# v spread over the key rows by transfers through DRAM, six banks in the ring, scores four tiles at a time

## The chip, the cores and the metric

One core of one Trainium2 chip runs the whole program. The metric is the device time of one execution in microseconds (us). TensorE multiplies matrices (PE in the rows, its weight loads PEld), VectorE (DVE), ScalarE (ACT) and GpSimd (POOL) do elementwise work, and SyncE (SP) issues all the transfers.

## The reference

32 sequences of 128 tokens with 512 features go through two layers. The first is cross attention with 32 query heads and 8 key heads of 16 features; the second is a linear-recurrence layer (RWKV) with 32 heads of 16 features and a feed-forward part. Cut to what matters:

```python
# layer 0
q = x @ Wq + bq;  k = ctx @ Wk + bk;  v = ctx @ Wv + bv
scores = einsum('bkgld,bksd->bkgls', q, k) / sqrt(16) + mask
out = einsum('bkgls,bksd->bkgld', softmax(scores), v)
x = layernorm(out @ Wo + bo + x) * gamma + beta
# layer 1: token shift, low-rank mixes, then
w = exp(-exp(time_decay + tanh(x5[1] @ decay_w1) @ decay_w2))
r, k, v = x5[3] @ Wr.T, x5[0] @ Wk.T, x5[2] @ Wv.T;  g = silu(x5[4] @ Wg.T)
def step(s, rkvw):                       # over 128 tokens
    a = k_t[:, :, :, None] * v_t[:, :, None, :]     # per head 16 x 16
    out = einsum('bhk,bhkd->bhd', r_t, u * a + s)
    return a + w_t[:, :, :, None] * s, out
att = groupnorm(outs);  x = x + (att * g) @ Wo.T
x = x + sigmoid(xr @ Wfr.T) * (square(relu(xk @ Wfk.T)) @ Wfv.T)
```

## The kernel before, in words

The batch is cut into 16 groups of two sequences (T = 256 tokens together). The work of a group is cut into steps such as `score.4` or `outer.7`; each engine has a written-out list of its steps (`PE_ORDER`, `ACT_ORDER`, `POOL_ORDER`, `DVE_ORDER`, lines 121 to 158), and runs the list once in each round. A step with `+1` or `+2` belongs to the group that entered one or two rounds earlier, so attention of one group, recurrence of the one before it, and output and feed-forward part of the one before that lie side by side. There are 16 + 2 rounds. Engines wait for one another by semaphores; within an engine the list is the order.

The recurrence keeps, for every head, a 16 x 16 state. 128 partitions hold 8 heads x 16 key rows (a chunk, four of them); along the free axis lie value columns d and the 256 tokens. A unit is one chunk and four value columns, so there are 16 units in a group. A unit goes through a slot of `st`, 128 x 1024, of which there are four:

- `spread` (TensorE, L717): v of one value column and head must stand in all 16 key rows of the head. A matmul with a 0/1 matrix `sel` does it. It runs in a faster number type that keeps fewer bits, so v is split into two parts: ScalarE writes the rounded v to `v_hi` (L979), VectorE the rest to `v_lo` (step `proj_v`, L1276), and eight matmuls a unit add both in `bank_pair`, two of the eight PSUM banks. Unit u's spread waits until the product of unit u-1 has read the pair.
- `outer` (VectorE, L1215): `st` slot = pair x k. `first` (ScalarE, L1027) writes the incoming state into the first column of each sequence.
- `scan` (VectorE, L1226, four scans), `weigh` (L1236, times r), then `reduce` (TensorE, L740), which sums over key rows for two units at once and counts `summed`. With that count the two slots are free.
- `readout` (L1244, L1246) adds the bonus term r·k·u·v; v for it is put together from both parts by GpSimd (L1089). `rk` is its step too (L1085).

The attention: `score.n` (L566) makes two score tiles in two PSUM banks on two sets of 32 rows of the array, four matmuls; VectorE takes each tile's row minima (L1173), ScalarE the exponential (L862), `turn_p` turns it (L575), `values` multiplies (L585), `inverse`, `flip`, `share`, `gather` and `project` finish. `low`, `low_rank`, `mix` (L1267 on VectorE, L1102 on GpSimd), `tdecay`, `decay` make the five mixes; `proj_r`, `proj_k`, `proj_v`, `proj_g` (L696) project them.

PSUM: `psum_jobs` hands the banks of `RING` (0, 1, 2, 4) out in the order of TensorE's list; bank 3 holds the attention's value sums, bank 7 the readout, and the pair is the rest. A step that writes a bank waits until its last reader is through. SP's transfers stand in `turn`: in each round `load_c`, `load_s` 0 and 1, `store`, `bring`, `load_s` 2, `save`, `load_m`, `load_x`, `load_t`, `load_s` 3.

Of the kernel before, what the change touches and what calls it, by code (L numbers as in the profile page):

```python
# [55 lines left out]
SLOTS = 4  # L56
# [65 lines left out]
reduce.4+2 spread.12+2 low_rank.0+1 spread.13+2 key.0 reduce.5+2 tdecay.0+1 spread.14+2 low_rank.2+1 proj_r.0+1  # L122
spread.15+2 decay.0+1 proj_v.0+1 proj_k.0+1 spread.0+1 reduce.6+2 decay.1+1 value.0 spread.1+1 reduce.7+2 query.0
spread.2+1 var.0+2 proj_r.1+1 score.0 rstd.0+2 query.1 score.2 spread.3+1 proj_g.0+1 proj_g.1+1 turn_p.0 turn_p.1
turn_p.2 reduce.0+1 spread.4+1 score.4 out.0+2 turn_p.3 score.6 spread.5+1 turn_p.4 out.1+2 values.0 reduce.1+1
turn_p.5 score.8 spread.6+1 proj_v.1+1 turn_p.6 flip.0 proj_k.1+1 turn_p.7 turn_m.0+2 score.10 share.0 spread.7+1
# [6 lines left out]
state.0+1 state.1+1 key.0 first.14+2 tdecay.0+1 proj_v.0+1 decay.0+1 first.15+2 proj_r.0+1 first.0+1 proj_k.0+1  # L133
decay.1+1 first.1+1 square.1+2 query.0 first.2+1 proj_r.1+1 state.2+1 score.0 score.1 state.3+1 query.1 score.2
proj_g.0+1 proj_g.1+1 turn_p.0 first.3+1 score.3 turn_p.1 row2.0+2 turn_p.2 first.4+1 score.4 turn_p.3 norm2.0+2
score.5 score.6 first.5+1 turn_p.4 score.7 norm2.1+2 first.6+1 turn_p.5 row0.0 apply2.0+2 score.8 apply2.1+2
first.7+1 flip.0 proj_v.1+1 score.9 turn_p.6 proj_k.1+1 turn_p.7 turn_m.0+2 share.0 score.10 turn_p.8 score.11
turn_p.9 score.12 turn_p.10 score.13 score.14 turn_p.11 score.15 turn_m.1+2 turn_p.12 turn_p.13 flip.1 turn_p.14
turn_p.15 share.1 first.8+1 norm0.0 apply0.0 first.9+1 norm0.1 first.10+1 norm1.0 apply0.1 first.11+1 ffn_k.0+2
norm1.1 apply1.0 ffn_k.1+2 apply1.1 ffn_r.0+2 square.0+1 turn_n.0 turn_n.1 ffn_r.1+2 row1.0 low.0 first.12+1  # L140
keep_row.0 first.13+1
# [3 lines left out]
norm0.0+1 rk.2+2 affine0.0+1 norm0.1+1 affine0.1+1 norm1.0+1 norm1.1+1 mix.0+1 mix.1+1 mix.2+1 mix.3+1 rk.3+2 rk.0+1  # L145
mix.4+1 negate.0 norm2.0+2 rk.1+1 norm2.1+2 bias.0 bias.1
# [3 lines left out]
outer.12+2 mix.0+1 mix.1+1 outer.13+2 scan.12+2 mix.2+1 mix.3+1 outer.14+2 readout.2+2 weigh.12+2 outer.15+2  # L150
scan.13+2 scan.14+2 proj_v.0+1 weigh.13+2 scan.15+2 weigh.14+2 outer.0+1 weigh.15+2 mix.4+1 value.0 outer.1+1
readout.3+2 scan.0+1 var.0+2 score.0 outer.2+1 score.1 weigh.0+1 groupnorm.0+2 score.2 scan.1+1 outer.3+1 score.3
proj_g.0+1 weigh.1+1 scan.2+1 proj_g.1+1 scan.3+1 weigh.2+1 score.4 score.5 outer.4+1 out.0+2 scan.4+1 score.6
weigh.3+1 score.7 outer.5+1 out.1+2 scan.5+1 score.8 readout.0+1 score.9 inverse.0 outer.6+1 weigh.4+1 proj_v.1+1
scan.6+1 score.10 score.11 weigh.5+1 outer.7+1 score.12 score.13 gather.0 weigh.6+1 score.14 outer.8+1 score.15
# [16 lines left out]
LATEST = max(late for t in (PE_STEPS, ACT_STEPS, POOL_STEPS, DVE_STEPS) for _, _, late in t)  # L172


RING, READOUT = [0, 1, 2, 4], 7


def psum_jobs():

    jobs, turn = [], 0  # L180
    for name, n, late in PE_STEPS:
        keys = [(name, n)]
        if name == "low_rank":
            keys = [("mix", 2 * m + p) for p in range(2) for m in range(n, min(n + 2, len(MIX)))]
        elif name == "score":
            keys = [(name, n), (name, n + 1)]
        elif name == "decay":
            keys = [("decay", n)] + [("mix", 8 + m) for m in range(2 * n)]
        elif name == "rstd":
            keys = [("rstd", 0), ("rstd", 1)]  # L190
        elif name == "reduce":
            keys = []
            if n % 2 == 0:
                jobs.append((("readout", n // 2), READOUT, late))
        elif name in ("spread", "values"):
            keys = []
# [6 lines left out]
def build(nc, x, ctx, mask, w, out, x1):  # L203
    XB = Banks(psum_jobs())
    ctxs = ExitStack()
    with ctxs:
# [16 lines left out]
        sel = sb("sel", [4, P], F32R)  # L223
# [20 lines left out]
        v_hi, v_lo = sb("v_hi", [NC, T], F32R), sb("v_lo", [NC, T], F32R)  # L244
# [3 lines left out]
        st = sb("st", [SLOTS, DU * T])  # L248
# [135 lines left out]

        xg = x.rearrange("(g b) l e -> g l b e", b=NB)
# [11 lines left out]
        def _(sp):  # L397
            def load_c(g):
# [6 lines left out]
            def load_t(g):  # L405
# [4 lines left out]
            def load_m(g):  # L410
# [4 lines left out]
            def load_x(g):  # L415
# [11 lines left out]
            def save(g):  # L427
# [4 lines left out]
            def bring(g):  # L432
# [5 lines left out]
            def store(g):  # L438
# [7 lines left out]
            def turn(it):  # L446
                ahead = not isinstance(it, int) or it + 1 < G
                if ahead:
                    load_c(it + 1)
                if known(it):  # L450
                    load_s(it, 0)
                    load_s(it, 1)
                if known(it - 2):
                    store(it - 2)
                if known(it - 1):
                    bring(it - 1)
                if known(it):
                    load_s(it, 2)
                    save(it)
                if ahead:  # L460
                    load_m(it + 1)
                    load_x(it + 1)
                    load_t(it + 1)
                if known(it):
                    load_s(it, 3)
# [10 lines left out]
            sp.dma_start(nmask[:], mg[0]).then_inc(loaded_m.sem, 16)  # L476
            sp.dma_start(xin[:], xg[0]).then_inc(loaded_x.sem, 16)
# [966 lines left out]
```

## Time and profile before

| | |
|---|---|
| time, median of 3 | 2303.19 us (2302.08 to 2303.35) |
| profiled execution, its own time | 2301.0 us |
| its span | 2299.2 us |
| mean granted TensorE clock | 0.967 |
| busy: PE, PEld | 2141.9 us (93%), 1477.2 us (64%) |
| busy: DVE, ACT, POOL | 1952.8 (85%), 1260.4 (55%), 585.2 us (25%) |

The span runs from the first to the last instruction. Busy shares are means over all of it; the start loads weights, the end runs without attention. A matmul in full number type shows as two records, one in the faster type as one. PE's busy time is a union of overlapping records.

### The profile page before, as it was taken

To read this page: it belongs to the slowest core of one execution; us is meant where nothing else is said; L and a number is where in the kernel's file an instruction comes from. 1 tells how busy PE (TensorE), PEld (TensorE's weight loads), DVE (VectorE), ACT (ScalarE), POOL (GpSimd) and SP (SyncE) were. 2 spreads that over 40 slices of the span, in tenths; PEclk is the share of its full clock that TensorE was granted. 3 is DMA by queue.
4 is the path that set the end of the run, shared out by engine and by line. 5 is a ranking of instruction groups with operands and counts; after the bars stand their busy time and mean duration, and the time that the engine had idled before them with its cause. 6 is when DMAs were issued, how large, how long until landed. Compare 5 with 4: busy or idle time off the path is not lost. (4 is left out here: it accounts for less than half of the span.)

```text
span 2299.2 us, 41734 instructions
## 1 busy us (share of the span) xinstructions
PE 2141.9 (93%) x14176; PEld 1477.2 (64%) x14176; DVE 1952.8 (85%) x4863; ACT 1260.4 (55%) x4405; POOL 585.2 (25%) x700
## 2 busy tenths in 40 slices
PE   3698799999999999999999999999999999999866
PEld 2475576767666676767667676766767676666533
DVE  0258898989899898989989898999989899998982
ACT  1736374573838466383746648373755738374312
POOL 1131314222331422232141322224141222314200
PEclk7799899999999999999999999999999999999977
DMA  7100101001010100001010100101010010100000
GB/s 268 35 7 20 31 11 49 11 11 41 11 50 11 49 11 31 21 11 50 11 49 11 48 3 11 50 11 50 11 49 1 11 50 11 50 2 29 1 19 10
DMA packets 48978, 69.88 MB, mean 30 GB/s; under 512 B 20512, under 2 KB 26656, under 8 KB 48768
## 3 DMA queue, kind: packets, MB, share of 16 engines
q1 hardware_dynamic: 48768, 67.21, 8.9%
q8 instruction: 115, 1.88, 0.3%
q14 instruction: 95, 0.78, 0.1%
HBM read 50.42 MB, written 16.78 MB: 29 GB/s over the span
## 5 line engine op out<-in xcount | busy, mean ns | idle before, releaser
L1226 DVE TENSOR_TENSOR_SCAN st<-ws,st 128x256 f32<-128x256 f32 x1024 | 637.4, 686 | 0.1
L862 ACT ACTIVATE probs_or_mixes<-probs_or_mixes,least 128x128 f32<-128x128 f32 x1024 | 398.9, 403 | 117.4 <-DVE least L1173 116.3
L1215 DVE TENSOR_TENSOR st<-bank_pair,kT 128x1016 f32<-128x1016 f32 x256 | 308.0, 1203 | 88.0 <-PE bank_pair L717 88.0
L1236 DVE TENSOR_TENSOR st<-st,rT 128x1024 f32<-128x1024 f32 x256 | 317.9, 1243 | 0.0
L1173 DVE CUSTOM_DVE_ANT_0 probs_or_mixes<-bank,nmask 128x128 f32<-128x128 f32 x1024 | 231.1, 285 | 100.5 <-PE bank L566 76.0
L1108 POOL TENSOR_SCALAR rstd<-rstd 128x1 f32<-128x1 f32 x96 | 26.5, 276 | 1098.4 <-ACT cin L895 600.1
L1102 POOL TENSOR_TENSOR probs_or_mixes<-probs_or_mixes 128x512 f32<-128x512 f32 x160 | 190.1, 1218 | 341.4 <-DVE probs_or_mixes L1267 341.4
L862 ACT ACTIVATION_READ_ACCUMULATOR probs_or_mixes<-probs_or_mixes,least 128x1 f32 x1024 | 206.4, 202 | 0.0
L717 PE MATMUL bank_pair<-v_hi,sel 32*128 32x256 f32 x1024 | 193.8, 339 | 10.9 <-DVE st L1215 10.6
L717 PE MATMUL bank_pair<-v_lo,sel 32*128 32x256 f32 x1024 | 166.6, 286 | 0.0
L717 PEld LDWEIGHTS bank_pair<-v_hi,sel 32*128 32x128 f32 x1024 | 114.5, 185 | 72.3 <-issue 35.4
L575 PE MATMUL bank<-consts,probs_or_mixes 128*128 128x128 f32 x1024 | 154.7, 282 | 4.4 <-ACT probs_or_mixes L873 2.2
L575 PEld LDWEIGHTS bank<-consts,probs_or_mixes 128*128 128x128 f32 x1024 | 114.1, 142 | 61.7 <-issue 39.3
L740 PE MATMUL bank<-st,consts 128*32 128x256 f32 x2048 | 140.6, 393 | 13.7 <-DVE st L1236 13.6
L873 ACT ACTIVATE probs_or_mixes<-bank 128x512 f32<-128x512 f32 x256 | 148.8, 598 | 7.2 <-PE bank L585 4.6
L566 PE MATMUL bank<-kbd,inputs_turned 32*128 32x256 f32 x1024 | 147.1, 403 | 5.7 <-DVE least L1173 3.3
L552 PE MATMUL bank<-inputs_turned,wq 128*128 128x256 f32 x512 | 120.6, 389 | 25.5 <-DVE least L1173 25.5
L1267 DVE SCALAR_TENSOR_TENSOR probs_or_mixes<-bank,cols,probs_or_mixes 128x256 f32<-128x256 f32 x320 | 129.2, 470 | 12.3 <-PE bank L653 10.8
L609 PE MATMUL bank<-wo,probs_or_mixes 128*128 128x512 f32 x256 | 118.4, 605 | 14.5 <-DVE probs_or_mixes L1195 14.1
L1085 POOL TENSOR_TENSOR rk<-rT,kT 128x256 f32<-128x256 f32 x64 | 93.1, 1454 | 146.7 <-issue 138.6
L696 PE MATMUL bank<-probs_or_mixes,wr 128*128 128x256 f32 x512 | 119.9, 388 | 7.4 <-DVE probs_or_mixes L1267 7.4
L792 PE MATMUL bank<-last_stage,fk 128*128 128x256 f32 x512 | 120.2, 389 | 6.5 <-DVE last_stage L1328 6.5
(150 smaller groups left out, 4216.3 us busy)
## 6 DMA issues: line engine op xcount, KB each, us to landing
inputs_turned<-in_ctx_turned SPq DMA_DIRECT2D x16, 512.0 KB, 3.6
inputs_turned<-in_x_turned SPq DMA_DIRECT2D x16, 512.0 KB, 4.6
xin<-in_x SPq DMA_DIRECT2D x16, 512.0 KB, 3.7
x<-xin SPq DMA_DIRECT2D x16, 512.0 KB, 4.1
keep<-x SPq DMA_DIRECT2D x16, 512.0 KB, 3.6
out<-keep SPq DMA_DIRECT2D x32, 256.0 KB, 2.0
wo<-in_wo SPq DMA_DIRECT2D x2, 1024.0 KB, 11.3
nmask<-in_mask SPq DMA_DIRECT2D x16, 128.0 KB, 4.1
```

The costliest lines, as they stand in the source:

```text
L566: last = mm(ps[m][0][:, ci * 2 * L:(ci + 1) * 2 * L], qT[r, 2 * cp + ci, b, :], kbd[r, b, :, :], start=True, stop=True)
L575: last = tr(ps[:, j * P:(j + 1) * P], pr[:, n % 4, j, :], ident)
L717: last = mm(pair[:, s, k * T:(k + 1) * T], sel[r, d % 4, :], part[r, c, :], start=part is v_hi, stop=part is v_lo)
L740: last = mm(ps[32 * (d // 4):32 * (d // 4) + 32, 0:T], ebase[:, o:o + 32], st[:, u % SLOTS, n * T:(n + 1) * T], start=m == 0 and k == 0, s ...
L862: last = fn(pr[:, n % 4, j, :], pr[:, n % 4, j, :], ACT.Exp, bias=least[:, n, j:j + 1], scale=-1.0, accum_out=rsum[:, n, j:j + 1])
L873: fn(pT[:, n % 4], ps[:].rearrange("p (j t) -> p j t", j=4), ACT.Copy).then_inc(free, 1)
L1102: tt(v, v, xnT[:, 2 * p:2 * p + 2, :, 1:], ALU.add).then_inc(mixed.sem, 1)
L1173: last = nc.vector.tensor_tensor_reduce(pr[:, n % 4, j, :], ps[:, j * P:(j + 1) * P], nmask[:, n // 8, :], 1.0, BIG, ALU.add, ALU.min, lea ...
L1215: tt(dst, src, over(kv, DU, 1), ALU.mult).then_inc(outer.sem, 1)
L1226: last = nc.vector.tensor_tensor_scan(v, ws[:, c].rearrange("p b t -> p (b t)"), v, 0.0, ALU.mult, ALU.add)
L1236: tt(v, v, over(rT[:, u // PER, :], DU, 1), ALU.mult).then_inc(weighed.sem, 1)
L1267: last = stt(out=x5[:, k % 4, c], in0=ps[:, q * T:(q + 1) * T].rearrange("p (b t) -> p b t", b=NB), scalar=col("maa", f * NC + c), in1=sx[ ...
```

## The change

v is kept once, in full type, in `vT` (128 x 4 x 256), written by ScalarE alone. SP saves each half of it to DRAM (`v_rows`) in four transfers (`save_v`), and for each unit reads it back into the slot, each head's four rows repeated over its 16 partitions (`spread` on SP). The product then works in place in the slot, and ScalarE's first columns are written after the transfer has landed. Slots become five, with a pitch of 1028 columns, and the transfer lands at columns 1 to 1024. The value columns of a chunk change their order, and the constants with it. `sel` is loaded straight to its own buffer. The pair's two banks join the ring. The score step makes four tiles in four banks. All step lists are new, and SP has one as well; TensorE waits for all four pieces of v's centred weights in `low` of the first group.

```diff
-SLOTS = 4
+SLOTS = 5
+PITCH = DU * T + 4
-RING, READOUT = [0, 1, 2, 4], 7
+RING, READOUT = [0, 1, 2, 4, 5, 6], 7
 PE_ORDER = """
+low_rank.0+1 key.0 low_rank.2+1 tdecay.0+1 proj_r.0+1 proj_v.0+1 proj_k.0+1 decay.0+1 decay.1+1 reduce.6+2 value.0
+reduce.7+2 query.0 var.0+2 proj_r.1+1 score.0 query.1 rstd.0+2 proj_g.0+1 turn_p.0 turn_p.1 proj_g.1+1 score.4
+out.0+2 turn_p.2 turn_p.3 out.1+2 values.0 reduce.0+1 turn_p.4 turn_p.5 score.8 turn_p.6 turn_p.7 reduce.1+1 flip.0
+values.1 turn_p.8 proj_v.1+1 turn_p.9 turn_p.10 turn_m.0+2 score.12 proj_k.1+1 turn_p.11 share.0 turn_p.12 turn_m.1+2
+reduce.2+1 turn_p.13 values.2 turn_p.14 project.0 turn_p.15 flip.1 share.1 values.3 reduce.3+1 project.1 ffn_k.0+2
+ffn_r.0+2 ffn_k.1+2 ffn_r.1+2 reduce.4+1 turn_n.0 turn_n.1 ffn_v.0+2 ffn_v.1+2 low.0 reduce.5+1
 DVE_ORDER = """
+mix.1+1 outer.13+2 mix.2+1 weigh.12+2 mix.3+1 readout.2+2 outer.14+2 outer.15+2 scan.13+2 scan.14+2 scan.15+2
+weigh.13+2 weigh.14+2 weigh.15+2 mix.4+1 readout.3+2 value.0 outer.0+1 outer.1+1 var.0+2 score.0 outer.2+1 score.1
+scan.0+1 score.2 score.3 groupnorm.0+2 scan.1+1 outer.3+1 proj_g.0+1 scan.2+1 score.4 proj_g.1+1 score.5 weigh.0+1
+out.0+2 weigh.1+1 outer.4+1 score.6 score.7 weigh.2+1 scan.3+1 out.1+2 weigh.3+1 score.8 score.9 inverse.0 score.10
+outer.5+1 score.11 outer.6+1 scan.4+1 scan.5+1 weigh.4+1 readout.0+1 score.12 score.13 scan.6+1 score.14 weigh.5+1
+score.15 gather.0 outer.7+1 weigh.6+1 scan.7+1 weigh.7+1 inverse.1 project.0 shift2.0+2 gather.1 outer.8+1 scan.8+1
+project.1 outer.9+1 readout.1+1 outer.10+1 outer.11+1 weigh.8+1 scan.9+1 weigh.9+1 outer.12+1 scan.10+1 scan.11+1
+shift.0 scan.12+1 weigh.10+1 weigh.11+1 ffn_v.0+2 ffn_v.1+2 mix.0
...
+SP_ORDER = """
+load_c.0 spread.7+2 save_v.1+2 spread.8+2 load_s.1+1 load_m.0 spread.9+2 spread.10+2 spread.11+2 spread.12+2 save.0+1
+load_s.2+1 spread.13+2 load_x.0 spread.14+2 load_t.0 spread.15+2 store.0+3 bring.0+2 load_s.3+1 save_v.0+1 spread.0+1
+spread.1+1 spread.2+1 spread.3+1 spread.4+1 load_s.0 spread.5+1 spread.6+1
...
+            def save_v(g, p):
+                wait(sp, outer.sem, outer.after(g - 1, 2 * PER * (p + 1)))
+                key = ("proj_v", p)
+                sp.wait_ge(emptied[XB.of(key)], XB.through(key, g))
+                for c in (2 * p, 2 * p + 1):
+                    for half in range(2):
+                        sp.dma_start(v_rows[c, :, half].rearrange("m (k t) -> m k t", k=2),
+                                     vT[64 * half:64 * half + 64, c, :]).then_inc(v_saved[p].sem, 16)
+
+            def spread(g, u):
+                c, p = u // PER, u // (2 * PER)
...
+                sp.wait_ge(v_saved[p].sem, v_saved[p].after(g, 4))
+                wait(sp, summed.sem, summed.after(g, (u - SLOTS) // 2 + 1))
+                r = HC * (UNIT_D[u % PER][0] // 2)
+                src = v_rows[c, r:r + HC].rearrange("h s n -> h (s n)")
+                n = slot(g, u)
+                sp.dma_start(st[:, n, 1:DU * T + 1],
+                             src.unsqueeze(1).to_broadcast([HC, HD, DU * T])).then_inc(landed[n], 16)
...
             def score(g, n):
+                four = range(n, n + 4)
...
                 for ci in range(2):
-                    for m in (n, n + 1):
+                    for m in four:
...
-            def spread(g, u):
...
-                wait(pe, outer.sem, outer.after(g, u))
-                for k in range(2):
-                    for part in (v_hi, v_lo):
-                        for s in range(2):
...
             def first_state(g, u):
-                wait(act, summed.sem, summed.after(g, (u - SLOTS) // 2 + 1))
+                v_there(act, g, u)
...
             def outer_(g, u):
-                wait(dve, summed.sem, summed.after(g, (u - SLOTS) // 2 + 1))
-                dve.wait_ge(spreaded.sem, spreaded.after(g, u + 1))
+                v_there(dve, g, u)
...
-                tt(dst, src, over(kv, DU, 1), ALU.mult).then_inc(outer.sem, 1)
+                tt(dst, dst, over(kv, DU, 1), ALU.mult).then_inc(outer.sem, 1)
...
-            def proj_v(g, p):
...
-                tt(v_lo[:, both, :], ps[:].rearrange("p (c n) -> p c n", c=2), v_hi[:, both, :].bitcast(F32),
-                   ALU.subtract).then_inc(free, 1)
```

## Rows read from the trace of the kernel before

**Rows 1.** The page: engines (share of span, instructions); transfer queue (packets, MB, share of 16 engines).

```profile
PE 2141.9 (93%) x14176; PEld 1477.2 (64%) x14176; DVE 1952.8 (85%) x4863; ACT 1260.4 (55%) x4405; POOL 585.2 (25%) x700
...
q1 hardware_dynamic: 48768, 67.21, 8.9%
```

**Rows 2.** Timeline of SP: context loads, first and last of thirteen (start, us, operation).

```profile
323.52 0.34 SPq L403 DMA_DIRECT2D inputs_turned<-in_ctx_turned  x1
...
1914.34 0.34 SPq L403 DMA_DIRECT2D inputs_turned<-in_ctx_turned  x1
```

**Rows 3.** Busy time in one round: us, PE, PEld, DVE, ACT, POOL, clock, transfers.

```profile
986.37:1118.94 132.57, 130.77 (x886) 90.64 (x885) 121.59 (x306) 78.37 (x276) 36.24 (x44) 1.00 0.09 26
```

**Rows 4.** Waits of DVE in that round (us in total, times, longest).

```profile
DVE st L1215 <- PE bank_pair L717: 5.4, 2, 4.9
DVE probs_or_mixes L1173 <- PE bank L566: 3.2, 3, 1.3
DVE xin L1200 <- PE bank L609: 1.5, 1, 1.5
```

**Rows 5.** Busy time of L717 (spread) in that round: PE, PEld, clock, transfers.

```profile
986.37:1118.94 132.57, 14.30 (x128) 10.52 (x128) 1.00 0.09 26
```

**Rows 6.** Timeline of PE, one score step (start, us, count).

```profile
1107.74 0.76 PEld L566 LDWEIGHTS bank<-kbd,inputs_turned 32*128 32x128 f32 x8 [0.25 <-issue]
1107.77 1.13 PE L566 MATMUL bank<-kbd,inputs_turned 32*128 32x256 f32 x8
```

**Rows 7.** Busy time in that round of L566 (PE, PEld), then of L1276 (DVE).

```profile
986.37:1118.94 132.57, 9.05 (x64) 5.62 (x64) 1.00 0.09 26
...
986.37:1118.94 132.57, 1.34 (x2) 1.00 0.09 26
```

**Rows 8.** Groups of instructions: count, busy us and mean ns, idle before.

```profile
L1215 DVE TENSOR_TENSOR st<-bank_pair,kT 128x1016 f32<-128x1016 f32 x256 | 308.0, 1203 | 88.0 <-PE bank_pair L717 88.0
L1236 DVE TENSOR_TENSOR st<-st,rT 128x1024 f32<-128x1024 f32 x256 | 317.9, 1243 | 0.0
```

**Rows 9.** Timeline of DVE, turn of a round.

```profile
1187.17 3.19 DVE L1267 SCALAR_TENSOR_TENSOR probs_or_mixes<-bank,cols,probs_or_mixes 128x256 f32<-128x256 f32 x8
...
1192.19 1.57 DVE L1236 TENSOR_TENSOR st<-st,rT 128x1024 f32<-128x1024 f32 x1
1193.69 1.20 DVE L1215 TENSOR_TENSOR st<-bank_pair,kT 128x1016 f32<-128x1016 f32 x1
1194.81 4.85 DVE L1226 TENSOR_TENSOR_SCAN st<-ws,st 128x256 f32<-128x256 f32 x8
```

**Rows 10.** Transfers by name: count, KB each, median us from issue to landing.

```profile
inputs_turned<-in_ctx_turned SPq DMA_DIRECT2D x16, 512.0 KB, 3.6
inputs_turned<-in_x_turned SPq DMA_DIRECT2D x16, 512.0 KB, 4.6
...
out<-keep SPq DMA_DIRECT2D x32, 256.0 KB, 2.0
...
rows<-in_rows SPq DMA_DIRECT2D x1, 832.0 KB, 5.5
```

**Rows 11.** Timeline of SP: save of x1 and the load behind it.

```profile
1182.96 0.40 SPq L430 DMA_DIRECT2D x<-xin  x1
...
1187.31 0.38 SPq L419 DMA_DIRECT2D xin<-in_x  x1
```

**Rows 12.** Timeline of POOL, same stretch as rows 9.

```profile
1188.09 4.59 POOL L1102 TENSOR_TENSOR probs_or_mixes<-probs_or_mixes 128x512 f32<-128x512 f32 x4 [2.56 <-DVE probs_or_mixes L1267]
1192.63 1.72 POOL L1085 TENSOR_TENSOR rk<-rT,kT 128x256 f32<-128x256 f32 x1
```

**Rows 13.** Timeline of PE, same stretch: projection of v's first half.

```profile
1193.50 3.72 PE L696 MATMUL bank<-probs_or_mixes,wvv 128*128 128x256 f32 x16
```

**Rows 14.** Timeline of ACT, same stretch: its evacuation.

```profile
1197.26 0.60 ACT L979 ACTIVATE v_hi<-bank 128x512 fp32r<-128x512 f32 x1 [11.14 <-PE bank L696]
```

**Rows 15.** One line of the code, L531 (key.0): ns min/median/max, first and last start.

```profile
L531 PE MATMUL bank<-inputs_turned,wk x128: 379/379/796, 17.4 to 1977.6; 128*128 128x256 f32 x128
```

**Rows 16.** Busy time in the round before the full ones and after them.

```profile
123.00:255.10 132.10, 108.77 (x728) 77.63 (x727) 94.44 (x252) 66.17 (x248) 35.72 (x38) 0.87 0.08 22
2111.10:2230.00 118.90, 97.67 (x586) 64.83 (x580) 111.81 (x171) 27.29 (x78) 23.89 (x24) 0.88 0.04 14
```

More of the change, by code:

```diff
@@ L121 @@
 PE_ORDER = """
[L122 to L126, printed above, removed]
@@ L134 @@
[L134 to L138, printed above, removed]
@@ L139 @@
-turn_p.15 share.1 first.8+1 norm0.0 apply0.0 first.9+1 norm0.1 first.10+1 norm1.0 apply0.1 first.11+1 ffn_k.0+2
-norm1.1 apply1.0 ffn_k.1+2 apply1.1 ffn_r.0+2 square.0+1 turn_n.0 turn_n.1 ffn_r.1+2 row1.0 low.0 first.12+1
-keep_row.0 first.13+1
+key.0 tdecay.0+1 first.14+2 first.15+2 proj_r.0+1 proj_v.0+1 proj_k.0+1 decay.0+1 square.0+2 decay.1+1 keep_row.0+1
+state.2+1 square.1+2 query.0 proj_r.1+1 first.0+1 score.0 first.1+1 query.1 score.1 score.2 proj_g.0+1 score.3
+first.2+1 first.3+1 turn_p.0 proj_g.1+1 turn_p.1 first.4+1 score.4 score.5 norm2.0+2 turn_p.2 turn_p.3 state.3+1
@@ L151 @@
[L151 to L155, printed above, removed]
@@ L444, in wload @@
                 sp.dma_start(dst, src).then_inc(loaded_w[n], 16)
[L446 to L465, printed above, removed]
+            def save_v(g, p):
[8 more added lines that the diff above has]
+                c, p = u // PER, u // (2 * PER)
+                if first_group(g) and u == 0:
+                    sp.wait_ge(scaled, 1)
+                sp.wait_ge(v_saved[p].sem, v_saved[p].after(g, 4))
[5 more added lines that the diff above has]
+                             src.unsqueeze(1).to_broadcast([HC, HD, DU * T])).then_inc(landed[n], 16)
+            does = dict(load_c=load_c, load_t=load_t, load_m=load_m, load_x=load_x, load_s=load_s, save=save,
+                        bring=bring, store=store, save_v=save_v, spread=spread)
             load_c(0)
@@ L475, in _ @@
                 wload(1, dst[:], w[n].rearrange("(c p) n -> p c n", p=P))
-            sp.dma_start(nmask[:], mg[0]).then_inc(loaded_m.sem, 16)
-            sp.dma_start(xin[:], xg[0]).then_inc(loaded_x.sem, 16)
+            load_m(0)
+            load_x(0)
             wload(2, w1[:], w["w1"].rearrange("(c p) n -> p c n", p=P))
@@ L493, in _ @@
             for it in range(G + LATEST):
-                turn(it)
+                for name, n, late in SP_STEPS:
+                    g = it - late
+                    if known(g) and not (g == 0 and name in FIRST):
+                        does[name](g, n)
             sp.wait_ge(stored.sem, stored.after(G, 0))
@@ L991, in v_free @@
             def v_free(g, p):
[L992 to L993 removed]
+                wait(act, v_saved[p].sem, v_saved[p].after(g - 1, 4))
+                stand(act, "act")
+                wait(act, diag.sem, diag.after(g - 1, 2 * p + 2))
             def proj_g(g, p):
```

154 lines of the change are left out of this document (64 added, 90 removed).

## The prediction

> **What bounds the kernel now.** I read the engines' totals first, then cut out one steady round. The totals put TensorE at 93% and VectorE at 85% of 2299.2 us [rows 1]; both are averages over a start, a middle and an end. The loads of the turned context, one in each round, stand 132.57 us apart from 323.52 to 1914.34 us [rows 2], so the middle repeats exactly: twelve such distances. The reader is to see in one of these rounds that TensorE is busy 130.77 of 132.57 us at granted clock 1.00, and VectorE 121.59 [rows 3]. So TensorE is the bound by 9 us, and VectorE stands close behind it. VectorE's idle time in the round is named in the waits: 5.4 us for the spread of v (L717), 3.2 us for scores (L566), 1.5 us for the attention's projection [rows 4]. What leaves TensorE therefore shortens the round, but only down to VectorE's own work.
>
> **TensorE's side.** The spread of v over the key rows leaves it. All 128 matmuls of a round hold it 14.30 us [rows 5]. The score step now issues eight matmuls on four sets of 32 rows where it issued four on two sets. One step of now shows 8 records in 1.13 us, its weight loads 8 in 0.76 us [rows 6]; the round's 64 records take 9.05 us [rows 7]. Four steps in place of eight: if four sets run beside one another as two do now, a step of 16 records still takes 1.13 us, and 8 x 1.13 - 4 x 1.13 = 4.5 us go; but 16 weight loads at 0.76 / 8 = 0.095 us would take 1.52 us, and then 9.05 - 4 x (1.52 + 0.38) = 1.5 us go; if nothing overlaps, 0. I take 3 us. TensorE after: 130.8 - 14.3 - 3 = 113.5 us, between 112 and 118.
>
> **VectorE's side.** The subtraction that made v's low part goes: 1.34 us a round [rows 7]. The product of v and k read PSUM and took 1203 ns for 1016 columns; it now reads SBUF, as the weighing by r does, 1243 ns for 1024 [rows 8]. Eight columns are 8 ns of that (1203 / 1016 each), so +32 ns a product, x16 = +0.5 us. The row of an undisturbed product is 1.20 us, but one weighing, beside a GpSimd product, took 1.57 us [rows 9, 12]; two of sixteen products hit so would cost +0.7 us. Bounds -0.2 to +1.5, taken +0.5. GpSimd loses the joining of v's two parts, of which VectorE notices nothing. So VectorE needs 121.6 - 1.3 + 0.5 = 120.8 us, and about 1 us between instructions stays (132.57 - 121.6 - 10.1 of named waits): a floor of 121.8 us. The scan and the reduction of minima keep their durations.
>
> So the bound changes hands: VectorE 121.8, TensorE about 113.5. The round can lose at most 132.6 - 121.8 = 10.8 us, not the 17 us that TensorE loses.
>
> **What becomes late next.** The price of v moves to SP and the transfers. Each of 16 units a round is 128 x 1024 f32 = 512 KB written in one transfer, from 8 rows of 4 KB repeated 16 times. The nearest rows: 512 KB loads land 3.6 to 4.6 us after issue, 256 KB stores 2.0, and the one load that repeats a row over all partitions, 832 KB, 5.5 [rows 10]; after the save of x1, 512 KB, the load that waits for it comes 4.35 us behind [rows 11]. I take 4.5 for a spread and 3 us for the four 64 KB saves, bounds 3.6 to 6.8 and 2.0 to 4.35. The upper 6.8 is the same 512 KB at half the width: 256 KB more cost 3.6 - 2.0 = 1.6 us, so 512 KB at half rate 3.6 + 2 x 1.6. An issue holds SP 0.4 us [rows 11]: 24 more of them, 10 us of a round; the queue is otherwise empty most of the time. The traffic is 256 x 512 KB = 134 MB; 67 MB now take 8.9% of the transfer engines' span [rows 1], so three times as much takes about 30%: no bound.
>
> SP works in order, so I walked its new list for what stands ahead of each spread. load_x waits for the landing of x1's save and for the last use of xin, and spreads 14 and 15 are behind it and load_t; their products follow shift, low, low_rank and the first mixes, over 10 us later: hidden. load_m is ahead of spread 9, and the score that it waits for lies over 15 us ahead of product 9: hidden. store and bring wait for VectorE's ffn_v, before mix.1: hidden unless that comes late. Most slots are freed early as well: from weighing 1, which ends reduce.0, to product 5 VectorE has 11 us of other work, from weighing 7 to product 11 some 12, and the way round is reduce 1.1, issue 0.4, landing 4.5 = 6.0 us.
>
> The tight place is the turn of the round, twice. (1) v's first half. From VectorE's mix.3: GpSimd adds it (ends 2.3 us later now [rows 9, 12]), TensorE projects v in 3.7 us [rows 13], ScalarE evacuates in 0.6 [rows 14], then four issues 1.7, landing 3, issue 0.4, landing 4.5: 16.2 us until product 0 may start, 14.3 to 19.9 by the bounds. VectorE has, between mix.3 and product 0 in its new order, two products 2.3, three scans 7.2, three weighings 3.4, mix.4 1.6 [rows 8, 9], and readout.2, readout.3 and value, 2.1 together = 16.6 us. Just covered; 3.3 us late at the upper bound. (2) The slot of product 1, freed by reduce.6 after weighing 13: 6.4 us of other work against 6.0, and 1.9 us late at the upper bound. ScalarE, which writes the first columns after the landing, is in the same race: a late landing holds the exponentials queued behind it, and so turn_p and the value matmuls on TensorE, which has 8 us of idle to give. Also, reduce.7 comes behind value.0 on TensorE, so readout.3 may wait 1 to 2 us. I put VectorE's waits at 2.7 us a round, where it had 10.1 while it was not the bound and TensorE, then the bound, had 1.8: round 124.5 us, saving 8.1.
>
> **The edges.** Key.0 starts from 17.4 to 1977.6 us [rows 15]; with rounds of 132.57 the third starts near 255 and the sixteenth ends near 2111, so 14 rounds are full: 14 x 8.1 = 113 us. The round before them (123 to 255) holds TensorE 108.8 and VectorE 94.4 of 132.1 us [rows 16]: neither is full; I take -5. The round after, without attention, is VectorE's already, 111.8 of 118.9 us [rows 16], and loses no score; 1.3 us of v's low part and the waits for L717 go, transfers without attention work to hide them come: +2, bounds -5 to +10. At the start TensorE now waits until all four pieces of v's centred weights are copied, 0.6 us each as other evacuations of this size: +1.5. Together 2299.2 - 113 - 5 + 2 + 1.5 = 2184.7 us of span. The profiled execution took 2301.0, so 1.8 outside the span: 2186.5; the median shown, 2303.2, is 2.2 above that. I predict 2189.
>
> **Rivals.**
> A. VectorE runs almost without a gap: round 122.4. For it: TensorE was idle 1.8 of 132.57 us when it was the bound. Against: it had no transfers in its way. 14 x 10.2 = 143 instead of 113: 2159.
> B. Four-tile scores and a blocked ScalarE cost rhythm. A score step needs four banks of six empty at once, and all four fill at its end, so VectorE waits 1 to 2 us for a step's first tile, four times a round; and the exponentials wait for its minima. Round 128: 14 x 4.6 = 64, so 2238.
> C. The transfers run at half width and land after 6.8 us. The row of 832 KB in 5.5 us speaks against, the 4.6 us row neither way. Product 0 is then late by 16.2 + 2.3 - 16.6 = 1.9 us, product 1 by 1.9 more at most, the first columns on ScalarE likewise: 3 us more a round, 127.5: 14 x 5.1 = 71, so 2231.
> The Trainium skill, page "DMA: Bandwidth & Descriptors", section "Why a DMA increments its semaphore by 16 and not by 1", states that a transfer runs on the largest number of engines up to 16 that divides the slowest dimension of both sides; the source's slowest dimension here is 8 heads, which would be half the engines. That is C by a rule; no transfer of this trace has such a source.
> D. Slower than before: TensorE's clock. It is granted 1.00 in the round because TensorE never rests; with 113.5 busy of 124.5 us it rests 9% of the time. Where it does so now, in the round from 123 (82% busy) and the one from 2111 (82%), the granted clock is 0.87 and 0.88 [rows 16], a mixture of 2.4 and 1.2 GHz. If the new round fell to c, TensorE would need 113.5 / c + 1.8 us: 122 at 0.945, where it begins to bind, and 132.6 at 0.868, the point from which nothing is gained. At 0.85 the round is 135.3, +2.8 x 14 = +39: 2342. Against: the fall there goes with pauses of several us and more; I expect rests of 1 to 2 us, spread out.
>
> **Chances.** Forecast (round 123.3 to 126.5) 0.49, A 0.13, B 0.16, C 0.10, D 0.12, of which 0.09 beyond its point of no gain and 0.03 at it. So faster 0.88, within 0.2% (4.6 us, about what a measurement of this kernel can tell from no change) 0.03, slower 0.09. Range for 8 in 10: from below A, 2150, to 2258, beyond B and C; the forecast's own is 2172 to 2217.
>
> **What would show it.** Rounds 123.3 to 126.5 us apart, VectorE over 119 us busy in one and TensorE near 114 at clock 1.00; no L717; score matmuls under 7 us a round; the product at 1.20 to 1.25 us; spreads landing 4 to 5 us after issue; VectorE's few waits behind the landing of v. Wrong if the product waits for transfers more than 6 us a round, if TensorE stays over 120 us busy or its clock falls below 0.95 in a round, or if products beside GpSimd take 1.4 us and more.

## The result: slower by 4.7%

The changed kernel takes 2410.97 us (median of 4 runs, 2407.85 to 2413.53) against 2302.64 us (2302.01 to 2303.35) for the kernel before: ratio 1.047, 95% interval 1.0452 to 1.0488. I had forecast 2189, in a range of 2150 to 2258, with a chance of 0.09 for slower. The profiled execution took 2409.67 us with a span of 2407.8, 108.6 more than before.

The page of the changed kernel, totals and transfer queue, against [rows 1]:

```profile
PE 2029.2 (84%) x12128; PEld 1358.5 (56%) x12128; DVE 2037.3 (85%) x4831; ACT 1268.6 (53%) x4405; POOL 665.7 (28%) x635
...
q1 hardware_dynamic: 93824, 209.84, 34.3%
```

TensorE lost 113 us of work, as intended. VectorE, which was to lose some, has 84 us more. The loads of the turned context, first and last of thirteen, against [rows 2]:

```profile
324.54 0.34 SPq L415 DMA_DIRECT2D inputs_turned<-in_ctx_turned  x1
...
2003.09 0.34 SPq L415 DMA_DIRECT2D inputs_turned<-in_ctx_turned  x1
```

Twelve distances of 139.88 us on average instead of 132.57: 7.3 us more in each round, 102 us over the 14 full rounds, of the span's 108.6. So the loss sits in the steady round, and one round is enough to look at. Busy time in one (us, PE, PEld, DVE, ACT, POOL, clock, transfer share, GB/s), against [rows 3]:

```profile
1023.39:1163.56 140.17, 123.89 (x756) 83.29 (x756) 127.84 (x302) 78.91 (x275) 42.60 (x39) 0.95 0.35 89
```

No engine is full. VectorE, the fullest, is busy 127.84 us and idle 12.3. The reader is to see two faults there: 127.84 where I had 120.8, and 12.3 where I had 3.7. The waits of VectorE, then of ScalarE, in that round (us in total, times, longest), against [rows 4]:

```profile
DVE st L1203 <- DMA st<-v_rows: 7.2, 3, 2.8
DVE probs_or_mixes L1165 <- PE bank L586: 1.5, 2, 1.2
DVE keep L1303 <- PE bank L772: 1.0, 1, 1.0
...
ACT st L1025 <- DMA st<-v_rows: 6.0, 2, 4.5
```

**The idle part.** ScalarE evacuates the first half of v at 1112.75 to 1113.35. Then SP's saves and spreads and VectorE's products, each from the timeline of its engine (start, us, count; idle before and what ended it):

```profile
1113.42 3.21 SPq L465 DMA_DIRECT2D v_rows<-vT  x4
1118.12 6.93 SPq L478 DMA_DIRECT2D st<-v_rows  x5
...
1125.29 1.37 DVE L1203 TENSOR_TENSOR st<-st,kT 128x1016 f32<-128x1016 f32 x1
1129.44 1.22 DVE L1203 TENSOR_TENSOR st<-st,kT 128x1016 f32<-128x1016 f32 x1 [2.78 <-DMA st<-v_rows]
```

Five spreads are issued in one burst. The second product starts 4.15 us after the first, although VectorE was ready 2.78 us earlier: the transfers come in one by one, 4.1 us apart, and 512 KB in 4.1 us is 128 GB/s. The windows over the burst have the same rate, and the transfer engines' share says why:

```profile
1120.00:1129.00 9.00, 9.00 (x85) 6.80 (x77) 6.48 (x11) 3.40 (x13) 5.08 (x5) 1.00 0.51 127
1129.00:1138.00 9.00, 9.00 (x63) 7.19 (x63) 8.19 (x32) 3.45 (x15) 0.00 (x0) 1.00 0.52 124
```

The share is the mean over the core's 16 transfer engines, and 0.51 with transfers queued throughout is what 8 of 16 would give. Everything behind a burst is late too; transfers by name (count, KB, median us from issue to landing), against [rows 10], where the first two took 3.6 and 4.6:

```profile
inputs_turned<-in_ctx_turned SPq DMA_DIRECT2D x16, 512.0 KB, 11.5
inputs_turned<-in_x_turned SPq DMA_DIRECT2D x16, 512.0 KB, 12.8
...
v_rows<-vT SPq DMA_DIRECT2D x128, 64.0 KB, 2.1
```

What a late spread does beyond the product is seen at the start of the round. Timelines of ScalarE, then of TensorE:

```profile
1034.21 0.22 ACT L1025 ACTIVATE st<-s 128x8 f32<-128x8 f32 x1 [4.46 <-DMA st<-v_rows]
1034.33 0.80 ACT L901 ACTIVATE cin<-keep,less,rstd 128x512 f32<-128x512 f32 x1
1035.03 0.39 ACT L861 ACTIVATE probs_or_mixes<-probs_or_mixes,least 128x128 f32<-128x128 f32 x1
...
1036.72 1.12 PE L595 MATMUL bank<-consts,probs_or_mixes 128*128 128x128 f32 x4 [4.42 <-ACT probs_or_mixes L861]
```

And two windows of the same place, columns as above:

```profile
1032.50:1036.50 4.00, 0.00 (x0) 0.00 (x0) 2.29 (x3) 2.29 (x10) 0.00 (x0) 0.95 0.51 160
1037.00:1041.00 4.00, 2.86 (x16) 2.09 (x15) 4.00 (x7) 3.95 (x13) 0.00 (x0) 0.50 0.12 36
```

The first column waits 4.46 us for its spread, the exponentials queue behind it on ScalarE, TensorE stands 4.42 us for them, and is then granted 0.50, the lower of its two levels, for some microseconds.

**The busy part.** Groups of instructions (busy, mean ns | idle before), against [rows 8]:

```profile
L1214 DVE TENSOR_TENSOR_SCAN st<-ws,st 128x256 f32<-128x256 f32 x1024 | 670.3, 721 | 1.4
L1203 DVE TENSOR_TENSOR st<-st,kT 128x1016 f32<-128x1016 f32 x256 | 351.0, 1380 | 108.3 <-DMA st<-v_rows 108.1
L1224 DVE TENSOR_TENSOR st<-st,rT 128x1024 f32<-128x1024 f32 x256 | 328.5, 1298 | 1.1
L1095 POOL TENSOR_TENSOR probs_or_mixes<-probs_or_mixes 128x512 f32<-128x512 f32 x160 | 226.5, 1449 | 273.7 <-DVE probs_or_mixes L1256 273.5
```

The durations of one line (ns min/median/max), the product of the kernel after:

```profile
L1203 DVE TENSOR_TENSOR st<-st,kT x256: 1186/1216/2277, 152.3 to 2333.2; 128x1016 f32<-128x1016 f32 x128
```

The same line of the kernel before, where the product read PSUM:

```profile
L1215 DVE TENSOR_TENSOR st<-bank_pair,kT x256: 1152/1206/1218, 145.0 to 2224.2; 128x1016 f32<-128x1016 f32 x128
```

Median against median the source in SBUF costs 10 ns. But before, no product out of 256 took over 1218 ns, and now they reach 2277; the mean is 1380. GpSimd's mixes went from 1218 to 1449 ns. The place is the turn of the round (VectorE, then GpSimd):

```profile
1105.70 4.21 DVE L1203 TENSOR_TENSOR st<-st,kT 128x1016 f32<-128x1016 f32 x2
1109.83 8.64 DVE L1214 TENSOR_TENSOR_SCAN st<-ws,st 128x256 f32<-128x256 f32 x12
1118.40 4.00 DVE L1224 TENSOR_TENSOR st<-st,rT 128x1024 f32<-128x1024 f32 x3
...
1096.76 12.08 POOL L1095 TENSOR_TENSOR probs_or_mixes<-probs_or_mixes 128x512 f32<-128x512 f32 x8 [14.61 <-DVE probs_or_mixes L1256]
1108.80 2.24 POOL L1071 TENSOR_TENSOR xin<-xin,rows 128x512 f32<-128x512 f32 x1
```

Two products that take 2.4 us alone take 4.2 beside GpSimd's mixes. Instruction by instruction, the two engines finish in turn there: a mix at 1106.73, product 14 at 1107.80, the next mix at 1108.84, product 15 at 1109.91, GpSimd's sum of x and bias at 1111.04, the first scan at 1111.58. The product's place in the list is not the reason. In the trace of before, 46 of the 256 products overlap a mix by over 0.1 us, more than any other GpSimd instruction, and take 1195 to 1206 ns; in the trace of after 42 do and take 1202 to 2187, median 2108.

### The profile page after: what moved, and what is told of

It is laid out like the page before. It is cut to its first block and busy times, and to the rows that moved or that the text cites. A ratio compares the mean times of both kernels' runs of the same rounds, so it can differ in the third digit from the quotient of the medians.

```text
span 2407.8 us, 37895 instructions
## 1 busy us (share of the span) xinstructions
PE 2029.2 (84%) x12128; PEld 1358.5 (56%) x12128; DVE 2037.3 (85%) x4831; ACT 1268.6 (53%) x4405; POOL 665.7 (28%) x635
## 3 DMA queue, kind: packets, MB, share of 16 engines
q1 hardware_dynamic: 93824, 209.84, 34.3%
## 5 line engine op out<-in xcount | busy, mean ns | idle before, releaser
L1214 DVE TENSOR_TENSOR_SCAN st<-ws,st 128x256 f32<-128x256 f32 x1024 | 670.3, 721 | 1.4
L1203 DVE TENSOR_TENSOR st<-st,kT 128x1016 f32<-128x1016 f32 x256 | 351.0, 1380 | 108.3 <-DMA st<-v_rows 108.1
L1095 POOL TENSOR_TENSOR probs_or_mixes<-probs_or_mixes 128x512 f32<-128x512 f32 x160 | 226.5, 1449 | 273.7 <-DVE probs_or_mixes L1256 273.5
L1101 POOL TENSOR_SCALAR rstd<-rstd 128x1 f32<-128x1 f32 x96 | 56.4, 587 | 807.0 <-ACT cin L894 609.5
L715 PE MATMUL bank<-probs_or_mixes,wvv 128*128 128x256 f32 x512 | 130.0, 412 | 39.3 <-POOL probs_or_mixes L1095 39.3
L1256 DVE SCALAR_TENSOR_TENSOR probs_or_mixes<-bank,cols,probs_or_mixes 128x256 f32<-128x256 f32 x320 | 131.1, 473 | 33.7 <-ACT ws L971 21.0
L586 PE MATMUL bank<-kbd,inputs_turned 32*128 32x256 f32 x1024 | 90.7, 476 | 65.2 <-DVE gT L1265 33.1
L715 PE MATMUL bank<-probs_or_mixes,wkk 128*128 128x256 f32 x512 | 140.7, 436 | 0.0
L715 PEld LDWEIGHTS bank<-probs_or_mixes,wvv 128*128 128x128 f32 x512 | 103.5, 207 | 61.7 <-POOL probs_or_mixes L1095 45.7
L772 PE MATMUL bank<-wo,att 128*128 128x512 f32 x256 | 135.4, 680 | 3.0 <-DVE att L1295 3.0
L715 PEld LDWEIGHTS bank<-probs_or_mixes,wkk 128*128 128x128 f32 x512 | 112.9, 224 | 28.7 <-issue 9.8
L791 PE MATMUL bank<-last_stage,fk 128*128 128x256 f32 x512 | 119.1, 387 | 6.5 <-DVE last_stage L1310 6.5
```

Source lines behind the costliest of these rows:

```text
L715: last = mm(ps[:, q * T:(q + 1) * T], wt[:, e, c * P:(c + 1) * P], x5[:, k % 4, e], start=e == 0, stop=e == NC - 1)
L772: last = mm(ps[:], att[:, c, b * P:(b + 1) * P], big["wo2"][:, c, :], start=c == 0, stop=c == NC - 1)
L1095: tt(v, v, xnT[:, 2 * p:2 * p + 2, :, 1:], ALU.add).then_inc(mixed.sem, 1)
L1203: tt(dst, dst, over(kv, DU, 1), ALU.mult).then_inc(outer.sem, 1)
L1214: last = nc.vector.tensor_tensor_scan(v, ws[:, c].rearrange("p b t -> p (b t)"), v, 0.0, ALU.mult, ALU.add)
L1256: last = stt(out=x5[:, k % 4, c], in0=ps[:, q * T:(q + 1) * T].rearrange("p (b t) -> p b t", b=NB), scalar=col("maa", f * NC + c), in1=sx[ ...
```

## The experiments

Two theories stood against each other at first. T: the spreads' rate, half the engines, makes the round; without their length it falls by the waits of VectorE and more. G: VectorE's own work has grown through GpSimd, and sets a new floor whatever the transfers do. A third, O, blames the new order and the four-tile scores; the time should then stay high with short transfers too. Round times below are means over eight rounds of the profiled execution, since single rounds differ by some 2 us; the kernel after has 139.9 so counted, the one before 132.6. Ratios are to the kernel before, on the same chip.

**e1_tiny: spreads of 64 columns.** The kernel after, but from the second use of each slot on a spread brings 64 of its 1024 columns, so most of v is left out.

```diff
-sp.dma_start(st[:, n, 1:DU * T + 1], src...)
+w_ = DU * T if UNITS * g + u < SLOTS else 64
+sp.dma_start(st[:, n, 1:w_ + 1], src[:, 0:w_]...)
```

> The changed kernel with each spread cut to its first 64 of 1024 columns (after the first use of a slot); 15/16 of v is left out, all waits stay. Round of the changed kernel: 140 us, 127.9 of it VectorE busy, 11 in waits. Theory T (transfers: 4.1 us each at 127 GB/s on half of the engines, queued in bursts): the waits behind st<-v_rows on VectorE (7.2 us a round) and ScalarE (6.0) go, round 129 to 132, time 2260 to 2310. Theory G (GpSimd stretches VectorE's two-input work): VectorE busy stays near 128 a round, so the round can't go below 129. If instead the transfers' writes stretch VectorE, busy falls to 121 as well and the time to 2200. Theory O (the new order and four-tile scores cost it): over 2370.

Measured: 2261.51 us (2260.56 to 2267.3), ratio 0.9826 (0.9812 to 0.9841), round 130.6.

```profile
1103.87:1233.71 129.84, 118.21 (x756) 79.78 (x756) 127.25 (x302) 78.65 (x275) 41.51 (x39) 1.00 0.12 35
```

The spreads' length costs 9.3 us a round and 149 us in all; that alone turns the sign. The round is now 2 us shorter than that of the kernel before, and theory O, which asked for over 2370, is out as the main cause. In this round TensorE's clock is back at 1.00 and its busy time at 118.2. VectorE, though, is busy 127.25 us as before, with 1.7 us of waits: traffic into the slots had nothing to do with its longer instructions, and G's floor is real.

**e2_wide: the same bytes on 16 engines.** Each half of v is saved twice, side by side, so that the slowest dimension of a spread's source counts 16 rows, each repeated 8 times. It costs 8 more saves of 64 KB a round.

```diff
-src = v_rows[c, r:r + HC].rearrange("h s n -> h (s n)")
...
-src.unsqueeze(1).to_broadcast([HC, HD, DU * T])
+src = v_rows[c, r:r + HC].rearrange("h q s n -> (h q) (s n)")
...
+src.unsqueeze(1).to_broadcast([2 * HC, HD // 2, DU * T])
```

> v saved twice side by side (8 saves of 64 KB a half instead of 4), so that the source of a spread has 16 rows repeated 8 times instead of 8 repeated 16 times. Theory T with the slowest-dimension rule: transfers run on all 16 engines, share in a burst 1.0 instead of 0.5 and 250 GB/s instead of 127, landing 2 us earlier and bursts twice as fast: 2290 to 2340 in spite of 4 more saves at 0.62 us of issue. If the rate is set by the repeated rows in DRAM: still 127 GB/s and 2410 to 2430. Theories G and O: 2395 to 2415.

Measured: 2282.1 us (2269.59 to 2288.82), ratio 0.992 (0.9892 to 0.9948), which is better than the 2290 to 2340 expected of theory T. One round, and a window over a burst of spreads:

```profile
1102.26:1232.16 129.90, 118.21 (x756) 79.78 (x756) 126.54 (x302) 78.70 (x275) 40.62 (x39) 1.00 0.40 99
...
1193.00:1204.00 11.00, 11.00 (x91) 8.41 (x89) 9.26 (x22) 2.69 (x8) 4.90 (x4) 1.00 1.00 228
```

What is left in that round of VectorE's wait for transfers:

```profile
DVE st L1204 <- DMA st<-v_rows: 1.4, 1, 1.4
```

Share 1.00 and 228 GB/s where the kernel after had 0.51 and 127: the source's eight rows were the limit. This round is as long as the one shown with almost no transfer, with every byte still moved, but it is one of the shortest. Over eight rounds this execution, the fastest of its four, has 131.1 us against 130.6 in e1_tiny, and that of e11_wide_again below, the slowest of its five, 132.1. So the width gives back 8 to 9 of the 9.3 us a round, and by the medians 2282 against 2262 some 20 us (0.9%) of the transfers' cost stay. A spread still lands a median of 6.0 us after its issue, for at full width too it stands in a queue:

```profile
st<-v_rows SPq DMA_DIRECT2D x256, 512.0 KB, 6.0
```

**e3_aligned** asks whether the destination, which starts one column into a slot, costs rate: data from column 7 with a pitch 4 wider, so that every transfer writes at a multiple of 32 bytes.

```diff
-sp.dma_start(st[:, n, 1:DU * T + 1],
+sp.dma_start(st[:, n, AT + 1:AT + DU * T + 1],      # AT = 7, PITCH = DU * T + 8
```

> Slot data begins at column 7, so that each spread writes from column 8, a multiple of 32 bytes, and the pitch is 1032; nothing else. If the destination shifted by 4 bytes is what holds an engine at 16 GB/s instead of the 22 of the weight loads, a transfer takes 3.0 us instead of 4.1 and the time is 2350 to 2380. If not, 2405 to 2415 (T by half width, G and O alike).

Measured: 2403.86 us (2400.82 to 2414.82), ratio 1.0448 (1.0422 to 1.0473), round 139.8. It is no more than 0.3% better than the kernel after, its interval overlapping; alignment is not the cause. **e6_wide_aligned**, the same two edits together:

> Two copies of v side by side (16 engines) and the destination at a multiple of 32 bytes. Since alignment alone gave 0.3%, theory T expects 2265 to 2290, as the wide run. If alignment counts once all 16 engines are on, the burst's rate rises over 240 GB/s and the time goes under 2262, the time with transfers cut to a sixteenth.

Measured: 2277.8 us (2271.73 to 2283.63), ratio 0.9891 (0.9869 to 0.9914), an interval that overlaps that of e2_wide.

**e4_gpsimd_light: G by itself.** Five kinds of GpSimd operations (mixes, r times k, x plus bias, and the two of the affine step) work on one column instead of 256 or 512, so their results are left out; the transfers stay as in the kernel after.

```diff
-tt(v, v, xnT[:, 2 * p:2 * p + 2, :, 1:], ALU.add)
+tt(v[:, 0, 0, 0:1], v[:, 0, 0, 0:1], xnT[:, 2 * p, 0, 1:2], ALU.add)
```

> GpSimd's mixes, r times k (after the first group), x plus bo and the affine steps are cut to one column each; the rest of those sums is left out, all waits stay. Theory G: the products at 1.38 us, weighings 1.30 and scans 0.72 fall to 1.21, 1.20 and 0.67, VectorE busy 121.5 a round instead of 127.9, and GpSimd's additions of the mixes no longer hold the projections: 2300 to 2330. Theory T alone: VectorE busy stays at 127 to 128, 2380 to 2400 from the shorter mixes.

Measured: 2322.67 us (2318.76 to 2327.42), ratio 1.0087 (1.007 to 1.0105), round 133.9. One round:

```profile
1124.35:1257.67 133.32, 122.13 (x756) 82.36 (x756) 119.64 (x302) 78.86 (x275) 18.82 (x39) 0.96 0.37 93
```

The groups of its scans and products:

```profile
L1214 DVE TENSOR_TENSOR_SCAN st<-ws,st 128x256 f32<-128x256 f32 x1024 | 616.0, 670 | 1.4
L1203 DVE TENSOR_TENSOR st<-st,kT 128x1016 f32<-128x1016 f32 x256 | 307.9, 1212 | 117.2 <-DMA st<-v_rows 117.1
```

VectorE's own instructions are untouched, and its busy time falls from 127.8 to 119.6 us, the product from 1380 to 1212 ns, the scans from 721 to 670. The wait for transfers stays (117.1 us against 108.1). So each cost is there without the other; whether they add up is the question of e7_tiny_light.

**e9_before_light: was that cost there before?** The same cut of GpSimd's work in the kernel before.

> The kernel before, with GpSimd's sums (mixes, r times k and the joining of v after the first group, x plus bo, affine) cut to one column. There TensorE is the bound, 130.8 of 132.6 us. Theory G: its VectorE busy falls too, from 121.6 by 1 to 3 us a round (weighings and scans only, the product reads PSUM and never took over 1218 ns), but not by the 8.2 us of the changed kernel; the time stays at 2280 to 2303. If VectorE's busy falls by 6 or more, the contention was there before and the change didn't add it.

Measured: 2287.02 us (2285.95 to 2287.93), ratio 0.9933 (0.9916 to 0.9949). VectorE is busy 120.37 us in a round instead of 121.59, and the round is 132.29, TensorE's still (130.75 us busy): 14 x 0.28 = 4 us of the 15.7 gained, so the other 12 lie in the rounds at the edges. So GpSimd took 1.2 us a round from VectorE before the change and 8.2 after it.

**e7_tiny_light: both costs out** (e1_tiny with e4_gpsimd_light; what both leave out is left out here).

> Both removed: spreads cut to 64 of 1024 columns, and GpSimd's sums cut to one column. If T and G are the two causes and add up (round 139.9; minus 10.1 by the first, minus 6.6 by the second), the round is 121 to 124 us and the time 2140 to 2185, where the prediction stood (round 124.5, 2189). If they cover the same waits, the round stays over 126 and the time over 2210.

Measured: 2212.71 us (2200.01 to 2215.57), ratio 0.9598 (0.957 to 0.9627), round 126.6. The sum of the two gains, 2140 to 2185, is missed; the result lies just inside the other case, the two covering the same waits in part (over 126 and over 2210). One round:

```profile
1077.34:1203.90 126.56, 119.31 (x756) 80.50 (x756) 119.10 (x302) 78.65 (x275) 18.99 (x39) 0.99 0.12 36
```

The waits of VectorE in it:

```profile
DVE probs_or_mixes L1241 <- ACT probs_or_mixes L940: 2.3, 1, 2.3
DVE probs_or_mixes L1166 <- PE bank L587: 1.4, 2, 1.1
DVE xin L1193 <- PE bank L630: 1.3, 1, 1.3
DVE last_stage L1274 <- PE bank L752: 0.7, 1, 0.7
DVE probs_or_mixes L1188 <- PE bank L606: 0.5, 1, 0.5
DVE dg L1234 <- issue: 0.5, 1, 0.5
```

The gains don't add: 9.3 and 6.0 us a round alone, 13.3 together. VectorE is busy 119.1 of 126.6 us and TensorE 119.3, and what is left of VectorE's idle time is small waits: four for TensorE, 3.9 us together, one of 2.3 for ScalarE.

**e5_pairs: two-tile score steps.** The kernel after, but with two steps of two tiles side by side in TensorE's list in place of one of four.

```diff
-score.0 ... score.4 ... score.8 ... score.12
+score.0 score.2 ... score.4 score.6 ... score.8 score.10 ... score.12 score.14
-four = range(n, n + 4)
+four = range(n, n + 2)
```

> The changed kernel with score steps of two tiles again (eight steps, each pair behind the other in TensorE's list at the place of the four). The four-tile step takes 6.12 us a round in the changed kernel, 4.58 with light transfers, against 9.05 of before. Theory: TensorE isn't the bound (123.9 of 140), so the time stays within 0.5% of the changed kernel, 2400 to 2420, with TensorE's score time back at 7 to 9 us. Rival O (the four banks at once cost the rhythm): 2380 or less, VectorE's waits at the score line down by over 1 us a round.

Measured: 2396.11 us (2393.45 to 2401.67), ratio 1.0409 (1.0393 to 1.0424), round 138.0. It is 0.6% faster than the kernel after, and so in neither of the two ranges expected (2400 to 2420; 2380 or less) but between them. In the round looked at, of 138.2 us, TensorE is busy 1.2 us longer (125.07), and VectorE's wait for scores falls from 1.5 us to 0.7, that for transfers from 7.2 to 6.1.

**e10_wide_pairs and e11_wide_again: a version that beats both.** e2_wide with e5_pairs, beside e2_wide itself once more on the same chip, as its runs had spread by 19 us.

> Two copies of v (16 engines) and two-tile score steps: only the score steps differ from the wide kernel. In the changed kernel the two-tile steps gave 0.6% (2396 against 2411). If that was the rhythm of banks (a four-tile step waits for its fourth bank while VectorE waits for its first tile), it holds here as well: 2255 to 2270 against the wide kernel's 2270 to 2289, and faster than before by 1.5 to 2%. If it came only from the waits for transfers, nothing is left of it: within 0.2% of the wide kernel.

> The wide kernel once more, unchanged, on the chip and beside the runs of the one above, since its four times spread from 2270 to 2289: median 2275 to 2285, the same spread.

Measured: e10_wide_pairs 2268.29 us (2257.15 to 2273.52), ratio 0.9836 (0.9812 to 0.9859); e11_wide_again 2278.59 us (2277.15 to 2288.18), ratio 0.9902 (0.9885 to 0.992). The wide spread's gain of about 1% is confirmed, and two-tile scores add 0.5% by the medians, 0.7% by the ratios; the two intervals don't touch. e10_wide_pairs computes all that the kernel before does. That the gain is there with wide spreads too fits the case named beforehand, that a four-tile step has to wait for its fourth bank; the bank waits were not cut out by themselves.

## Why the prediction was wrong

Three signs had been named that would make it wrong, and all three came: the product waits more than 6 us a round for transfers (7.2), TensorE stays over 120 us busy (123.9), products beside GpSimd take 1.4 us and more (4.21 for two). Forecast 124.5 us a round, measured 139.9: 15.4 us, of which the experiments place 9.3 on the spreads' length (e1_tiny; e2_wide gets most of it back) and 4.0 on GpSimd once these are out (e1_tiny against e7_tiny_light); 2.1 remain.

**The step that failed: "What becomes late next".** I priced a spread by a latency, 4.5 us from issue to landing, at worst 6.8, and asked of each tight place whether one spread makes it. The mechanism of half width stood there as rival C, at 2231. But the same text has five slots, which at the turn of the round are refilled at once, and a transfer of 4.1 us on half the engines is not only late by 2.3 us: five of them take 20 us. Product 1 was charged its own landing, not that of the spread ahead of it. In numbers: C had 3 us a round more than the forecast; the runs showed 9.3. And the 4.5 us were low even at full width, with 6.0 as the median in e2_wide. "The traffic takes about 30%: no bound" was right as a mean (34.3%) and beside the point; the bound is the share in a burst, 0.51, which half width makes the ceiling. The saves came out right in the sum, and partly by luck: four issues and a landing at 4.7 us, and 1113.42 to 1118.12 is 4.7, but of 3.21 for the issues, where I had 1.7, and 1.5 until the first spread, where I had 3.

The Trainium skill, page "DMA: Bandwidth & Descriptors", section "Why a DMA increments its semaphore by 16 and not by 1", was the rule cited in rival C; the trace agrees, 0.51 and 127 GB/s with eight rows, 1.00 and 228 GB/s with sixteen. I gave it a tenth because no row of before showed such a source. It deserved most of the chance: nothing in the trace spoke against it, the 832 KB row having a different source.

**The term "VectorE's side" was mis-sized.** Taken +0.5 us for the product, bounds -0.2 to +1.5; it measured 21.63 us a round against 19.25, +2.4. Beyond the product, the scans took 42.63 us against 39.71, with the edit leaving them alone. I had the row of the weighing of 1.57 us beside GpSimd [rows 9], and counted two products hit; in the trace of after 72 of 256 are over 0.1 us above the median, three to six of a round's sixteen. What it shows is an exclusion: an instruction with two operands in SBUF can be held for most of a GpSimd operation. The product was safe from it while one operand came from PSUM, 1206 ns at most beside a mix, and lost that in the change, with 2108 as the median there. The scans read two SBUF operands in both kernels; what changed for them is what they lie beside. Before, 36 of 1024 are over 0.1 us above the median, 15 of them beside a mix; after, 62 are, none beside a mix, but beside GpSimd's sum of x and bias (13), its affine step (30) and r times k (19). In e2_wide, with few waits for transfers left, 58 are, beside the same operations, so the new lists do it and not the late transfers. Product and scans are 4.8 of the 7.0 us that VectorE was off, and the weighings, 20.82 us a round against 19.86, one more; in e4_gpsimd_light 8.2 us go.

The Trainium skill states this, page "SBUF — State Buffer", section "Who interferes with whom": "A DVE instruction with two SBUF inputs contends with a GpSimd instruction that reads SBUF". The trace agrees, with 1218 ns as the longest of 256 products before and 2277 after. I had not weighed this rule, and it speaks against the change. The section also has transfers never contend with a compute engine, which e1_tiny bears out: VectorE is busy 127.25 us almost without them, 127.84 with them.

**TensorE's side** was right in direction and 4.7 us off in size: 118.2 us at clock 1.00, where I had 113.5. Score matmuls did better than thought, 4.58 us a round in e2_wide, from 9.05, and 6.12 in the kernel after, where part of them ran at the lower level. So spread and scores, by their own rows 14.3 and 4.5, should have taken 18.8 and took 12.6 from the engine's busy time. Busy time is a union of overlapping records, and the trace of before shows the rest: of the 14.30 us of spreads and 9.05 of scores in the round of [rows 3], 23.35 together, only 15.8 lie where no other matmul's record does, and of the spreads by themselves 7.5. The sum had counted them whole. It costs nothing while VectorE is at 127, and matters in e7_tiny_light, where both engines are at 119.

**Rival B** (four-tile scores), put at 3.5 us a round more, is there with 2 (e5_pairs), and about 10 us of the whole (e10_wide_pairs against e11_wide_again). **Rival D** (the clock) appeared as a consequence, not as a cause: 0.95 in the round, about where I had it begin to bind, and TensorE's busy time 123.9 us where it is 118.2 at 1.00, while VectorE had more to do still; in the round of e1_tiny it is 1.00 again. **Rival A** never had a chance beside the longer VectorE work.

**What held**: the bound changed hands to VectorE; the chain from a late first column through the exponentials to TensorE is the one I described, with 4.4 us where I had allowed for 8 us of idle; and the evacuation, 0.60 us. The edges did not: 6.3 us together (108.6 - 102.3) against -1.5 forecast, and what made them was not looked for.

**Left open.** The 24 us (1.1%) between e7_tiny_light (2212.7) and the forecast (2189) were not taken apart; its rounds, 126.6 us against 124.5, are long enough to hold them. Nor was the spread of 11 to 19 us between runs of one wide kernel, where the kernel before has 1 to 5. It goes with the granted clock: the runs of e11_wide_again have 0.957 at 2277.15 us and 0.947 at 2288.18, and in its trace a round of 130.0 us has 1.00 and one of 135.6 has 0.96. Which of the two makes the other is not shown. And what moving the mixes or products 13 to 15 apart would give, which is the obvious next step, was not tried.

## What to carry to other kernels

Price a transfer twice, by latency for one and by rate for as many as can be queued at once, and read the rate off the slowest dimension of both sides: eight rows meant half the engines, and a second copy of 512 KB a round made it all of them, for 2282 us in place of 2411. Before moving an operand of VectorE from PSUM to SBUF, look what GpSimd does at that time, and compare minimum, median and maximum of its instructions, not the mean. A step that frees the bounding engine is worth only the distance to the second one, and this one was 9 us away in a round of 132.

## What the runs showed of the hardware

- A transfer of 512 KB from 8 DRAM rows, each repeated over 16 partitions, used half of the transfer engines: 4.1 us, 127 GB/s, share 0.51. From 16 rows, each repeated 8 times: share 1.00, 228 GB/s. The start of the destination within 32 bytes changed at most 0.3%.
- VectorE and GpSimd hold each other up in both directions when VectorE's instruction has two operands in SBUF. A product of 1.21 us took up to 2.28, scans of 0.67 up to 1.77, and mixes of GpSimd 1.45 instead of 1.22 on average. Even this operation on a single column, in e4_gpsimd_light, took 2.06 us beside VectorE's weighings:

```profile
1214.23 2.06 POOL L1083 TENSOR_TENSOR rk<-rT,kT 128x1 f32<-128x1 f32 x1 [1.97 <-PE bank L724]
```

- With one operand in PSUM the product was not held: 1218 ns at most in 256, 46 of them beside mixes of GpSimd.
- Four sets of 32 rows run beside one another as two do: 64 score records in 4.58 us instead of 9.05 at clock 1.00, a factor of 2.0.
